# The shift of three norms, minus mean times reciprocal root, in one instruction of VectorE instead of two of GpSimd

## The reference

```python
x = x + attn_a(_layernorm(x))   # gated linear attention, 16 heads, then its own norm and a 512-wide gelu MLP
x = x + ffn(_layernorm(x))      # router, top 2 of 8 experts, expert product 256 x 256
x = x + attn_b(_layernorm(x))   # recurrence h = tanh(x_t B + h A^T) over 1024 steps, 16 states, out through C and W_out
x = x + ffn(_layernorm(x))      # the same experts again

def _layernorm(x, axis=-1, eps=1e-05):
    m = jnp.mean(x, axis=axis, keepdims=True)
    v = jnp.var(x, axis=axis, keepdims=True)
    return (x - m) / jnp.sqrt(v + eps)
```

## Time and profile before

| what | value |
|---|---|
| time, median of 3 runs | 1916.17 us (1913.14 to 1927.48) |
| span of the profiled execution | 1923.4 us |
| PE busy | 1801.3 us, 94% of the span |
| DVE busy | 1314.5 us, 68% |
| POOL busy | 1120.8 us, 58% |
| ACT busy | 917.9 us, 48% |
| mean granted TensorE clock | 0.957 of full speed |

### The profile page before, as it was taken

How to read it: one execution, slowest core, us unless ns; L and a number is a source line. 1 busy time by engine, 2 the same in 40 slices (tenths; PEclk the granted TensorE clock), 3 DMA queues, 4 the chain that set the end, 5 groups by cost and what they waited for, 6 DMA issues and landing times.

```text
span 1923.4 us, 47590 instructions
## 1 busy us (share of the span) xinstructions
PE 1801.3 (94%) x16264; PEld 1558.7 (81%) x16264; DVE 1314.5 (68%) x3881; ACT 917.9 (48%) x2535; POOL 1120.8 (58%) x1451
## 2 busy tenths in 40 slices
PE   4588999999999999999999999999999999998987
PEld 3467888888888888888888888888888888887765
DVE  4564667777777777777777777777777777776443
ACT  4444445555554555555445545554555555444321
POOL 4575566766666666556666766566567556654111
PEclk8797999999999999999999999999999999999778
DMA  4110000000000000000000000000000000000000
GB/s 128 34 31 16 23 29 24 22 22 22 22 27 27 26 23 17 27 16 27 27 27 22 24 20 22 21 27 27 27 22 17 27 16 28 23 24 6 3 9 11
DMA packets 71883, 47.79 MB, mean 25 GB/s; under 512 B 37616, under 2 KB 71056, under 8 KB 71696
## 3 DMA queue, kind: packets, MB, share of 16 engines
q1 hardware_dynamic: 70176, 45.28, 7.9%
q10 hardware_dynamic: 1648, 1.72, 0.3%
HBM read 30.21 MB, written 16.78 MB: 24 GB/s over the span
## 4 chain that ended last, share of the span: by engine, by line
PE 72%; POOL 15%; ACT 4%; DVE 4%; issue 3%; DMA 1%; POOLq 0%; SPq 0%; ACTq 0%; DVEq 0%
PE ps L996 52%; PE ps L1013 8%; POOL sx L442 7%; PE ps L1002 3%; PE ps L1021 2%; PE ps L1023 2%; POOL r L356 1%; PE ps L1033 1%; PE ps L1053 1%; POOL osq L438 1%; DVE yT L812 1%; POOL stage L460 1%; PE ps L1058 1%; ACT yT L673 1%; PE ps L1250 1%
## 5 line engine op out<-in xcount | busy, mean ns | idle before, releaser
L996 PE MATMUL ps<-we,yT 128*128 128x512 f32 x3072 | 849.3, 416 | 5.3 <-DVE yT L812 3.6
L996 PEld LDWEIGHTS ps<-we,yT 128*128 128x128 f32 x3072 | 558.2, 194 | 109.2 <-DVE yT L812 10.0
L505 ACT ACTIVATE hs<-ps 16x8 f32<-16x8 f32 x1024 | 177.8, 174 | 841.1 <-PE ps L1013 834.9
L1013 PEld LDWEIGHTS ps<-hs,aT 128*128 128x128 f32 x2048 | 354.8, 196 | 114.9 <-issue 62.5
L1013 PE MATMUL ps<-hs,aT 128*128 128x8 f32 x2048 | 333.2, 237 | 46.9 <-ACT hs L505 45.1
L384 POOL TENSOR_TENSOR part<-part 128x256 f32<-128x256 f32 x64 | 47.4, 741 | 413.3 <-ACT part L523 413.3
L760 DVE SCALAR_TENSOR_TENSOR stage<-ps,coef,stage 128x256 f32<-128x256 f32 x384 | 185.1, 482 | 143.6 <-POOL stage L386 114.9
L442 POOL TENSOR_TENSOR sx<-osq,cst 32x512 f32<-32x512 f32 x128 | 214.0, 1672 | 10.0
L760 DVE SCALAR_TENSOR_TENSOR acc<-ps,coef,acc 128x256 f32<-128x256 f32 x384 | 185.0, 482 | 26.8 <-POOL acc L386 12.6
L407 POOL TENSOR_TENSOR orstd<-omean,mhalf 128x32 f32<-128x32 f32 x32 | 174.0, 5438 | 2.7
L812 DVE TENSOR_TENSOR yT<-ps,yT 128x512 fp32r<-128x512 f32 x64 | 44.0, 691 | 109.8 <-ACT yT L684 64.6
(11 more groups left out here) (174 smaller groups left out, 3478.3 us busy)
## 6 DMA issues: line engine op xcount, KB each, us to landing
xin<-in_x SPq DMA_DIRECT2D x64, 128.0 KB
vrow<-vtok SPq DMA_DIRECT2D x32, 256.0 KB, 2.1
vx<-vrow SPq DMA_DIRECT2D x128, 64.0 KB, 2.0
xag<-in_x SPq DMA_DIRECT2D x64, 128.0 KB
out<-stage SPq DMA_DIRECT2D x64, 128.0 KB
stage<-in_experts SPq DMA_DIRECT2D x1, 2048.0 KB, 8.6
stage<-in_Wvg SPq DMA_DIRECT2D x1, 512.0 KB, 5.0
stage<-in_W SPq DMA_DIRECT2D x1, 512.0 KB, 4.5
```

Of the source, the lines that this page charges most:

```text
L505: return a.activation(hs[0:N, :, k], bt(ps[0:N, BANK["RB"], 0:TOK])[:, :, k], ACT.Tanh)
L996: ins = t.matmul(dst, left(lp, c), right(rp, c), start=(n == 1), stop=(n == 3 * chunks))
L1013: return t.matmul(bt(ps[0:NP, BANK["RB"], 0:TOK])[:, :, k], aT[:], hs[:, :, (k - 1) % TS], start=False, stop=True, skip_group_check=True)
```

## The change

GpSimd's `rstd` loses its last two instructions. VectorE gets a helper `shifted`, one instruction for both, `(mean * -1) * root`, behind a wait for the root. It is called at three places of VectorE's list: for `r` behind `onorm`, for `m2` behind the statistics of m1, and for `m1` behind `y0`.

```diff
-            def rstd(mv, buf, name, count, shift=False):
+            def rstd(mv, buf, name, count):
 
                 g.tensor_scalar(buf[:, 0, :], mv[:, :, 1], EPS, 1.0, ALU.add, ALU.mult).then_inc(sem(f"var_{name}"), 1)
                 pool.wait_ge(sem(f"var_{name}"), count)
                 g.tensor_tensor(buf[:, 1, :], buf[:, 0, :], mhalf[:, 0:TILES], ALU.pow).then_inc(sem(f"rstd_{name}"), 1)
-                if shift:
-                    pool.wait_ge(sem(f"rstd_{name}"), count)
-                    g.tensor_tensor(buf[:, 0, :], buf[:, 1, :], mv[:, :, 0], ALU.mult).then_inc(sem(f"mr_{name}"), 1)
-                    target = value(pool, count)
-                    pool.wait_ge(sem("pads_zero"), 1)
-                    pool.wait_ge(sem(f"mr_{name}"), target)
-                    g.tensor_scalar(buf[:, 2, :], buf[:, 0, :], -1.0, 1.0, ALU.mult, ALU.mult).then_inc(sem(f"shift_{name}"), 1)
...
-                    rstd(mv_r, rr, "r", c5, True)
+                    rstd(mv_r, rr, "r", c5)
...
-                    rstd(m2.mv, m2.r, "m2", c6, True)
+                    rstd(m2.mv, m2.r, "m2", c6)
...
-                    rstd(m1.mv, m1.r, "m1", c4, True)
+                    rstd(m1.mv, m1.r, "m1", c4)
...
+            def shifted(mv, buf, name, count):
+
+                target = value(dve, count)
+                dve.wait_ge(sem("pads_zero"), 1)
+                dve.wait_ge(sem(f"rstd_{name}"), target)
+                v.scalar_tensor_tensor(buf[:, 2, :], mv[:, :, 0], -1.0, buf[:, 1, :], ALU.mult, ALU.mult).then_inc(sem(f"shift_{name}"), 1)
...
                     v.tensor_tensor(onorm[:], ps[:, BANK["O"], :].rearrange("p (h v) -> p h v", v=DV),
                                          orstd[:].unsqueeze(2).broadcast_to([P, TILES * HEADS, DV]), ALU.mult).then_inc(sem("onorm"), 1)
+                if live(it, 5):
+                    shifted(mv_r, rr, "r", c5)
...
                     stats(m1.x, m1.st, m1.mv, "m1", c4)
+                if live(it, 6):
+                    shifted(m2.mv, m2.r, "m2", c6)
...
                     normed(y0, xin, mv_a[:, :, 0], ra[:, 6, :]).then_inc(sem("y0"), 1)
+                if live(it, 4):
+                    shifted(m1.mv, m1.r, "m1", c4)
```

More of the change, by code:

```diff
@@ L814, in body @@
             def body(it):
-                c1, c2, c3, c4, c6, c7 = (cnt(it, k) for k in (1, 2, 3, 4, 6, 7))
+                c1, c2, c3, c4, c5, c6, c7 = (cnt(it, k) for k in (1, 2, 3, 4, 5, 6, 7))
                 if live(it, 7):
```

## The result

The changed kernel takes 1984.62 us, the median of 4 runs (1978.43 to 1986.5), against 1915.45 us for the kernel before (4 runs). The ratio is 1.034, with a 95% interval of 1.030 to 1.038. It is slower by 69 us, where 1904 us had been forecast, with 1919 as the upper end of the range.

What follows compares the result with a forecast made beforehand. PE was taken as the bound, idling for m1's shift on POOL. Gains of 8.0, 1 and 2.2 us, 11 to 12 in all, were taken as 12 from 1916.2, giving 1904 us, range 1894 to 1919.

Steps and rivals of the forecast that it cites:

- What bounds the kernel: PE, busy 94%; in 16 passes it idles 1.25 us before step 7, waiting through `ym1` for POOL's shift of m1.
- Shift of m2, off POOL: On POOL behind m2's root: without L359 and L363 all later work moves up 0.58 us, m1's root ending about 1043.87.
- That time hangs on PE, not on POOL: On DVE behind `att` and `y0`: the shift of m1 starts at 1044.33 at the earliest, paced by PE's state update.
- POOL and DVE side by side: An added DVE instruction can slow a POOL instruction beside it by at most its own 0.16 us; cost nothing.
- the sum: Whole gain: 8.0 us from 16 passes, 1 from filling and draining, 2.2 from three lost low stretches; 11 to 12 us.
- B: Rival: low stretches go as PE's idle time shrinks, all 26 passes take 54.82, gain 16 to 19 us, 1897 to 1900; chance 0.27.
- D: Rival: DVE's new wait for m2's root makes `att` late; 1 us beyond the margin gives 1933; chance 0.07.
- C: Rival: nothing measurable, as `shifted`'s waits cost 0.5 us or ordinary passes turn low; 1913 to 1920; chance 0.16.
- 16 passes x 0.50 = 8.0 us: In the 16 passes with PE idle before step 7, m1's shift comes 0.50 us earlier, the middle of 0.42 to 0.58.
- the prediction's own lengths of a pass: PE's own length of a pass: 54.07 us at the full clock, 55.56 with a low stretch.

Runs made afterwards that it cites:

- the move of r: Against the kernel before, only the shift of r moved to VectorE, those of m2 and m1 left on GpSimd: 1920.88 us, ratio 1.000.
- `state` and `res` held back: Changed kernel plus one wait: GpSimd starts the decay of the state and the residual only when `y0` is written; 1908.26 us, 0.994 to the kernel before.
- m2 alone: Against the kernel before, only the shift of m2 moved to VectorE, those of m1 and r left on GpSimd: 1904.79 us, ratio 0.991.
- the run with the one-input forms: Changed kernel with GpSimd's `state` and `res` replaced by same-size instructions reading one tensor, leaving out decay and b2: 1927.43 us, 1.002 to the kernel before.

## Why the prediction was wrong

*What bounds the kernel* held: PE, and once a pass the way through POOL to `ym1`. Where PE waits, and that each 0.1 us of the shift of m1 is worth 0.1 us of PE, was borne out in both directions (PE's idle time 0.78, 1.52, 2.47 us with `y0` at 0.72, 1.47, 2.41).

*The step that failed* is in the part "Shift of m2, off POOL". It says that all that comes later on POOL moves up, and then follows only the root of m1. What stands behind the root was not followed: with the shift of m1 gone too, `state` starts not at 1045.04 but at 1077.58 - 33.83 = 1043.75, inside `y0`, which in the earlier trace rows runs from 1043.68 to 1044.41. `res` comes right behind it. The rows of before that were not followed:

```profile
1045.04 1.04 POOL L468 TENSOR_TENSOR state<-state,dec 128x512 f32<-128x512 f32 x1
1046.04 1.27 POOL L470 TENSOR_TENSOR res<-xag,b 128x512 f32<-128x512 f32 x1
```

With the prediction's own terms `state` comes to 1045.04 - 0.58 - 0.62 = 1043.84, within 0.1 us of what was measured. In the kernel before, the two shifts that were to be removed, and their gaps, had kept these instructions just out of `y0`'s way.

*"That time hangs on PE, not on POOL"*, said of the start of the shift of m1 at 1044.33, was the same error from the other side. It took `y0`'s 0.73 us as a property of the instruction. It hangs on POOL as soon as POOL streams beside it: the shift started at 1079.97 - 33.83 = 1046.14, 1.8 us later.

*"POOL and DVE side by side"* had the right subject and saw one of its two directions. It read from the earlier trace rows that a DVE instruction slows a POOL instruction, and capped this at the DVE instruction's own 0.16 us. That direction exists. The other one, a DVE instruction held for about as long as the POOL instruction lasts, was put at nothing, and it is the one that cost the 69 us. The Trainium skill, GPSIMD Engine Reference, section Specifications, names a contention of GpSimd with VectorE instructions in a 2-port perf mode or with two SBUF inputs, without saying there who waits or how long; I used it for a bound of 0.16 us instead of asking what else would meet. `y0` has one tensor input, so the half of this that I used did not point at it; no run here shows in which mode it runs. The trace of before held the answer in both directions, POOL's rows first, then DVE's of the same stretch:

```profile
1075.06 0.50 POOL L363 TENSOR_SCALAR rr<-rr 128x2 f32<-128x2 f32 x1 [0.16 <-POOL rr L359]
1075.52 1.29 POOL L418 TENSOR_TENSOR res<-res,xmid 128x512 f32<-128x512 f32 x1
```

```profile
1074.88 0.69 DVE L824 TENSOR_TENSOR_SCAN gcum<-cst,glog 128x256 f32<-128x256 f32 x1
1075.61 1.49 DVE L826 TENSOR_TENSOR grel<-gcum 128x256 f32<-128x256 f32 x1
```

L363, 0.19 us elsewhere, takes 0.50 and ends with the scan that had started before it. The subtraction L826, 0.42 us where it is free, starts just behind the residual L418 and takes 1.49; on the mean of all passes it is 1325 ns, and 425 after the move of r. Even the row that gave the new instruction its 0.16 us, has a maximum of 682 ns: that one ran beside a POOL addition of 128 x 256 (L386).

*What was right*: the length of the new instruction when it runs alone (0.16 forecast, 0.13 to 0.16 measured); `shifted` for m1 follows `y0` without idle time; m2's shift costs only the 0.13 us by which `att` is late, although it took 1.1 us instead of 0.16, because the wait for PE ahead of `att` covers the rest; r's shift costs nothing. With the collision taken away the sum came out: PE's idle time 0.78 for 0.75, a pass 54.85 for 54.82, 11 us gained for 12. A side forecast missed: POOL is busy 33 us less, not 50 (1120.8 to 1087.4), because the residual L418 and the instruction behind it (L423 in the kernel before) take 13 us longer in all at their new place beside DVE's gate instructions.

*The rivals.* B, low stretches becoming rarer with less idle time, is borne out in part, and never apart from the rest. From 260 to 1680 us the profiled executions have 10 low stretches with PE's idle time at 1.25 us, and 4 (two of them twice as long) and 5 with 0.78 and 0.76 (`state` and `res` held back; m2 alone), but again 6 with 0.2 and 9 with none; the changed kernel, with 2.47, has 25. Each count is of one execution. The Trainium skill, TensorE: Matmul & The Clock Gate, section What's actually happening, says that activity lifts the slow clock; the steps from 1.25 us of idle time to 2.47 and to 0.8 agree with it, the step from 0.8 to none does not. D named a slower outcome with a chance of 0.07, but by another way, the wait ahead of `att`; that cost 0.13 us. C did not occur. No rival was the one that happened: an instruction moved up by the removal of others, meeting one on another engine.

In the sum, the term "16 passes x 0.50 = 8.0 us" of gain was in truth 25 passes x 2.49 of loss: 1.6 us of it is added idle time (60.3 us over 25 passes, against 20.2 over 26), and the rest, some 0.9 us, is the low stretch that every pass now has. By the prediction's own lengths of a pass this is (1 - 10/26) x (55.56 - 54.07) = 0.9, an estimate.

## What to carry to other kernels

When instructions are taken off an engine, lay out the whole queue behind them at its new times and look at what each one will run beside, not only at the one whose result is waited for. A VectorE instruction's duration in a trace holds only for what GpSimd does beside it there, and the other way round; compare instructions of one form at several places of the trace, and where one takes three times as long, look for the other engine's instruction next to it. If two such instructions must share a stretch, put the one that is waited for first, and hold the other engine's work back with one wait: here that turned 3.4% slower into 2.0% faster.

## What the runs showed of the hardware

- A GpSimd instruction of 128 x 512 holds some VectorE instructions until about its end: a tensor_scalar from SBUF to SBUF of 128 x 256 went from 0.40 to 1.14 us, a scalar_tensor_tensor of 128 x 2 from 0.15 to 1.11, the scan of 128 x 256 from 0.69 to 1.52, a tensor_tensor of 128 x 256 with both inputs in SBUF (L826) from 0.42 to 1.33.
- The hold goes the other way too. GpSimd's L363 takes 0.50 us instead of 0.19 beside the scan, and 0.36 beside `y0` in the run with m2 alone; four of 52 additions of 128 x 256 (L386) in the kernel before take up to 1.44 us instead of 0.73, beside a VectorE tensor_tensor of 128 x 512 from SBUF. The engine that started later was the one held in most of these rows; where the starts lie 0.02 to 0.15 us apart it was at times the earlier one (L386, and `y0` in the run with the one-input forms). `res`, which starts before the second instruction of `y0`, hardly felt it (1.27 alone, 1.31 beside `y0`).
- Not held: VectorE's tensor_tensor with one input in PSUM and one in SBUF. With `state` and `res` held back, `dstate` and `xmid` run beside them, in 0.68 and 0.67 us, the same as where they run alone. L826 is a tensor_tensor too and is held; it has both inputs in SBUF. Nor are VectorE's statistics of 128 x 256, with one input in SBUF, held: 0.76 us for the two beside `res` there, 0.75 elsewhere.
- GpSimd's one-input form holds too, for its own, shorter time (0.62 and 0.65 us); and whether VectorE's two scalars come from memory or stand in the instruction makes no difference beside GpSimd (2.41 and 2.42 us for the two), though one such instruction alone takes 0.40 us with scalars from memory and 0.28 with numbers.
- That a shared way into SBUF is the cause is what the forms held and not held suggest, and the Trainium skill, GPSIMD Engine Reference, section Specifications, says that the two engines share their SBUF interfaces; no run here shows the way itself.
